# Where partial sums of activations are built, and in which places and order tiles are loaded, in a two-stage f32 matmul kernel

## The reference, cut to what matters

```python
w = weight[adapter_ids]                        # one 2048x2048 matrix for each of the 8 batches
x = x + einsum('bsi,boi->bso', x, w)           # called x1 below
h = einsum('bti,bir->btr', x, lora_A[slot])    # 16 columns
x = x + einsum('bti,oi->bto', x, W) + b + 2 * einsum('btr,bro->bto', h, lora_B[slot])
```

## Time and profile before

| | before |
|---|---|
| median of 3 runs (range) | 2672.59 us (2669.78 to 2679.78) |
| the profiled execution: its time, its span | 2670.25 us, 2668.5 us |
| PE busy | 2573.8 us, 96% of the span |
| DVE, ACT, POOL busy | 1664.3, 876.2, 1247.3 us |
| mean granted clock of PE | 0.988 |
| DMA traffic | 648.03 MB, 243 GB/s in the mean |

### The profile page before, as it was taken

One profiled execution on the slowest core, in us unless ns is written; L12 is line 12 of the kernel. 1 busy time (PEld: TensorE's weight loads), 2 busy tenths in 40 slices (PEclk: granted clock), 3 DMA queues, 4 the chain that ended last, 5 costly groups with the idle time before them and its releaser, 6 DMA issues.

```text
span 2668.5 us, 30970 instructions
## 1 busy us (share of the span) xinstructions
PE 2573.8 (96%) x11232; PEld 2118.8 (79%) x11232; DVE 1664.3 (62%) x1880; ACT 876.2 (33%) x1157; POOL 1247.3 (47%) x1484
## 2 busy tenths in 40 slices
PE   7999999989989999999989989999999999999998
PEld 6887878878878878878878868888888788788776
DVE  5454445444454354453433357899898887999996
ACT  3232232232232242232322324333333333333332
POOL 3333424434434343333322455555666665555665
PEclk9999999999999999999999989999999999999999
DMA  9888888999988878878967894554577955443665
GB/s 336 295 295 269 298 278 262 300 262 290 297 244 308 251 266 321 271 242 264 273 167 194 207 360 148 174 170 163 180 248 262 369 203 172 156 144 131 231 224 192
DMA packets 238155, 648.03 MB, mean 243 GB/s; under 512 B 30132, under 2 KB 46516, under 8 KB 238004
## 3 DMA queue, kind: packets, MB, share of 16 engines
q0 software_dynamic: 124672, 397.48, 46.0%
q1 hardware_dynamic: 113332, 248.57, 28.6%
HBM read 433.07 MB, written 212.86 MB: 242 GB/s over the span
## 4 chain that ended last, share of the span: by engine, by line
PE 86%; DMA 6%; DVE 5%; POOL 1%; issue 1%; ACT 1%; SPq 0%; DVEq 0%; ACTq 0%
PE bank L783 16%; PE bank L785 16%; PE bank L784 16%; PE bank L812 12%; PE bank L814 12%; PE bank L816 12%; DMA x_raw<-xT 3%; DVE x_lo L604 2%; DMA bm<-bs 1%; PE bank L768 1%; PE bank L830 1%; PE bank L769 1%; DVE w_lo L598 1%; DMA wl<-w1s 1%; DVE xc L682 1%
## 5 line engine op out<-in xcount | busy, mean ns | idle before, releaser
L783 PE MATMUL bank<-x_hi,w_hi 128*128 128x512 f32 x2048 | 802.4, 392 | 60.8 <-DVE x_lo L604 60.8
L366 POOL TENSOR_TENSOR wl<-wl 128x512 fp32r<-128x512 f32 x392 | 587.1, 1518 | 459.0 <-ACT wl L532 444.5
L784 PE MATMUL bank<-x_lo,w_hi 128*128 128x512 f32 x2048 | 801.0, 391 | 0.0
L785 PE MATMUL bank<-x_hi,w_lo 128*128 128x512 f32 x2048 | 800.8, 391 | 0.0
L812 PE MATMUL bank<-xc,wl 128*128 128x512 f32 x1568 | 614.9, 392 | 20.4 <-DVE h_mix L617 8.4
L814 PE MATMUL bank<-xc,wl 128*128 128x512 f32 x1568 | 612.2, 390 | 0.0
L816 PE MATMUL bank<-xc,wl 128*128 128x512 f32 x1568 | 611.9, 390 | 0.0
L486 ACT ACTIVATE w_hi<-w_raw 128x1024 fp32r<-128x1024 f32 x256 | 257.5, 1052 | 972.0 <-PE bank L785 961.3
L703 DVE TENSOR_TENSOR x_raw<-bank,x_raw 128x512 f32<-128x512 f32 x128 | 88.5, 691 | 690.3 <-PE bank L785 639.7
L783 PEld LDWEIGHTS bank<-x_hi,w_hi 128*128 128x128 f32 x2048 | 387.0, 189 | 144.0 <-DVE x_lo L604 47.3
L785 PEld LDWEIGHTS bank<-x_hi,w_lo 128*128 128x128 f32 x2048 | 387.0, 189 | 80.9
(11 more groups left out here) (47 smaller groups left out, 1674.4 us busy)
## 6 DMA issues: line engine op xcount, KB each, us to landing
w_raw<-w0T SPq DMA_DIRECT2D x256, 512.0 KB, 7.9
wl<-w1s SPq DMA_DIRECT2D x392, 256.0 KB, 2.7
xss<-x_raw POOLq DMA_DIRECT2D x256, 256.0 KB, 4.2
w1s<-q_raw POOLq DMA_DIRECT2D x196, 256.0 KB, 7.2
q_raw<-w1T POOLq DMA_DIRECT2D x96, 512.0 KB, 9.8
xq<-xss POOLq DMA_DIRECT2D x40, 1024.0 KB, 7.1
x1s<-x_raw POOLq DMA_DIRECT2D x128, 256.0 KB, 2.9
c<-x1s POOLq DMA_DIRECT2D x32, 1024.0 KB, 13.3
```

The costliest lines, as they stand in the source:

```text
L366: pool.tensor_tensor(w[:, 1], w[:, 1].bitcast(F32), w[:, 0].bitcast(F32), ALU.subtract).then_inc(wl_ready, 1)
L783: pe.matmul(sums[s][:], w_hi[s][:, k, :], x_hi[:, k, :], start=(k == 0), stop=False)
L784: pe.matmul(sums[s][:], w_hi[s][:, k, :], x_lo[:, k, :], start=False, stop=False)
L785: mm = pe.matmul(sums[s][:], w_lo[s][:, k, :], x_hi[:, k, :], start=False, stop=(k == KT - 1))
```

## The change

1. **x in nine places.** `x_raw` gets nine chunk places instead of eight (1024 more words per partition, taken from the unused `q_rest`). Chunk 0 of batch 1 is loaded at the start, and every later chunk one place earlier: chunk 7 of the next batch follows tile 13, and after tile 15 comes chunk 0 of the batch after that.
2. **The start.** SP issues all of batch 0's chunks, in turn with the first weights; the second table of slots and the bias follow the weights of tile 1, and POOL's first loads (LoRA A, W) wait for that table and for chunk 6.
3. **The outer sums.** Phase one writes each x1 tile once, and the tiles of the lower half (t >= 8) also negated (`x1n`, 64 stores). `xss` and its 320 writes (160 plain, 160 accumulating) are gone. In phase two each `load_xq` fetches a quadrant of x1, and for five of the seven outer products an accumulating DMA of another 1 MB (`add_xq`) adds the second quadrant, or its negative, into the same SBUF buffer. That makes 40 such loads, four for each of ten outer products; each waits, on POOL, until the plain load has landed, and is issued two pieces after it. Four of them come at the end of phase one.
4. **The border of the phases.** The loads of c0, c1, c2 are spread over pieces 6 to 32 instead of standing in bunches of four at pieces 5, 9 and 13; the last store of h and the waits behind it move from piece 8 to 10 and 17; DVE makes the last low part of h before its first addition into c; PE waits for it at piece m=2 of chunk 1, not at m=0. SP's first `wl` load waits for tile 113's sum as well, since the memory now overlaps `x_raw`.
5. **The end.** The last eight stores (256 KB each) are issued by SP (c0) and ACT (c2) instead of POOL.

The diff, cut:

```diff
-B_SUM = [S6, S7, S1, None, S3, None, S4]
+B_SUM = [(0, 1, False), (2, 3, False), (0, 3, False), (0, None, False), (1, 3, True), (3, None, False), (0, 2, True)]
...
+    XS = XC + 1
...
+    def xq_loads(outer):
+        return sum(1 + (B_SUM[i % OUTER][1] is not None) for i in range(outer + 1))
+
+    def x_rows(b, c):
+        place = (b * XC + c + XC - 1) % XS
+        return slice(place * KX, (place + 1) * KX)
...
+        C_LOADS = {6: (0, 0), 8: (0, 3), 11: (0, 1), 13: (0, 2), 18: (1, 0), 20: (1, 2), 22: (1, 1), 24: (1, 3),
+                   26: (2, 0), 28: (2, 2), 30: (2, 1), 32: (2, 3)}
...
@@ sync
+            b, t = place_of(SEQ // PER_GROUP - 1, 0, INNER_INTO[INNER - 1])
+            for m in range(Q):
+                sp.wait_ge(acc_free, (SEQ - 1) * Q + m + 1)
+                sp.dma_start(yT[b, t + m], c0[:, INNER_INTO[INNER - 1], m]).then_inc(y0_last, 16)
...
@@ gpsimd
+            def add_xq(outer, q):
+                group, o = divmod(outer, OUTER)
+                quad, negative = B_SUM[o][1:]
+                if quad is None:
+                    return
+                pool.wait_ge(xq_loaded[q], (xq_loads(outer) - 1) * 16)
+                b, t = group * 4 + quad % 2 * 2 + q % 2, quad // 2 * HALF + q // 2 * Q
+                source = x1n[b, t - HALF:t - HALF + Q] if negative else x1s[b, t:t + Q]
+                pool.dma_start(xq[q][:], source.rearrange("t p n -> p t n"),
+                               accum_op=ALU.add).then_inc(xq_loaded[q], 16)
...
                     pool.dma_start(x1s[b, t], x1_raw[s][:]).then_inc(x1_stored[s], 16)
-                    for i in BEGINS[quad]:
-                        pool.dma_start(xss[b // 4, i, b % 2, t % HALF], x1_raw[s][:]).then_inc(x1_stored[s], 16)
-                    for i in ADDS[quad]:
-                        pool.dma_start(xss[b // 4, i, b % 2, t % HALF], x1_raw[s][:],
-                                       accum_op=ALU.add).then_inc(x1_stored[s], 16)
-                    for i in SUBTRACTS[quad]:
+                    if t >= HALF:
                         negatives += 1
                         pool.wait_ge(x1_neg_done, negatives)
-                        pool.dma_start(xss[b // 4, i, b % 2, t % HALF], x1_neg[s][:],
-                                       accum_op=ALU.add).then_inc(x1_stored[s], 16)
-                    if b < NB - 1 and t % KX == KX - 1:
-                        load_x(b + 1, t // KX)
+                        pool.dma_start(x1n[b, t - HALF], x1_neg[s][:]).then_inc(x1_stored[s], 16)
+                    if t % KX == KX - 1:
+                        next_b, next_c = divmod(b * XC + t // KX + XS, XC)
+                        if next_b < NB:
+                            load_x(next_b, next_c)
...
                         for q in ((1, 3), (0,), (2,))[j - 3]:
                             load_xq(outer + 1, q)
-                if n == 5:
-                    for i in (0, 3, 1, 2):
-                        load_c(0, 0, i)
-                if n == 8:
-
+                if step == 1 and s >= 0 and outer < SEQ // INNER - 1 and j in (4, 5, 6):
+                    for q in ((1, 3), (0,), (2,))[j - 4]:
+                        add_xq(outer + 1, q)
+                if n == 10:
                     store_h(NB - 1)
+                if n == 17:
+
                     pool.wait_ge(h_stored, NB * 16)
...
@@ scalar
-                    act.wait_ge(xq_loaded[place], (s // INNER + 1) * 16)
+                    act.wait_ge(xq_loaded[place], xq_loads(s // INNER) * 16)
```

More of the change, by code:

```diff
@@ L94, in build @@
     x1s = scratch("x1s", (NB, NT, P, TOK))
-    xss = scratch("xss", (NB // 4, 5, 2, HALF, P, TOK))
+    x1n = scratch("x1n", (NB, HALF, P, TOK))
     w1s = scratch("w1s", (PER_GROUP, Q, P, Q, P))
@@ L98, in build @@
     bs = scratch("bs", (NB, 2, P, HALF * P))
-    def x1_writes(n):
-        quad = n % NT // HALF * 2 + n // NT % 4 // 2
-        return 1 + len(BEGINS[quad] + ADDS[quad] + SUBTRACTS[quad])
     def x1_stores(n):
-        return sum(x1_writes(i) for i in range(n % 2, n + 1, 2))
+        return sum(1 + (i % NT >= HALF) for i in range(n % 2, n + 1, 2))
+    def xq_loads(outer):
[3 more added lines that the diff above has]
+        return slice(place * KX, (place + 1) * KX)
     def xc_sums(until):
@@ L243, in piece, with place_of @@
             return q_raw[u % 3][:, which // 2, which % 2 * Q:(which % 2 + 1) * Q]
+        def place_of(group, quad, i):
+            return group * 4 + quad % 2 * 2 + i % 2, quad // 2 * HALF + i // 2 * Q
+        C_LOADS = {6: (0, 0), 8: (0, 3), 11: (0, 1), 13: (0, 2), 18: (1, 0), 20: (1, 2), 22: (1, 1), 24: (1, 3),
+                   26: (2, 0), 28: (2, 2), 30: (2, 1), 32: (2, 3)}
         q_store = [[(0, 0), (6, 1), (5, 3)], [(1, 3), (4, 2)], [(2, 0)], [(3, 1)]]
@@ L269, in _ @@
                                      .rearrange("a p k o -> (a p) k o")).then_inc(w_loaded[s][part], 16)
+                        if n == 0:
+                            for c in ((2, 3), range(4, XC))[part]:
+                                load_x_first(c)
+                    if n == 1:
+                        sp.dma_start(ids_sb[:, 1, :], ids1).then_inc(ids1_loaded, 16)
+                        sp.dma_start(bias_sb[:], bias).then_inc(bias_loaded, 16)
             def load_bm(i):
@@ L279, in _ @@
             sp.wait_ge(q_stored, UNITS * INNER * 16)
+            sp.wait_ge(x1_sum, TILES - NT + KX)
             for s in range(SEQ):
@@ L367, in wl_lo @@
                                    ).then_inc(wl_ready, 1)
-            for c in range(2, XC):
-                pool.dma_start(x_raw[:, c * KX:(c + 1) * KX], xT[0, c]).then_inc(x_first[c], 16)
-            pool.wait_ge(ids_loaded, 32)
+            pool.wait_ge(ids1_loaded, 16)
+            pool.wait_ge(x_first[XC - 2], 16)
             load_a(0)
             load_q(0)
+            load_x(1, 0)
             negatives = 0
@@ L447, in _ @@
                         pool.wait_ge(x1_stored[i], x1_stores(TILES - 2 + i) * 16)
-                if n in (9, 13):
-                    for i in (0, 2, 1, 3):
-                        load_c(0, (1, 2)[n // 13], i)
+                if n in C_LOADS:
+                    load_c(0, *C_LOADS[n])
                 if step == 1 and s >= 1:
@@ L469, in _ @@
                                                    ).then_inc(y_stored[quad][i], 16)
[L470 to L474, removed]
             for quad in range(4):
@@ L477, in _ @@
                     last = LAST[quad] == OUTER - 1 and INNER_LAST[i] == INNER - 1
-                    pool.wait_ge(y_stored[quad][i], (1 + (Q if last else 1)) * 16)
+                    pool.wait_ge(y_stored[quad][i], (1 if last else 2) * 16)
         @block.scalar
@@ L590, in _ @@
                     h_hi(NB - 1)
+            b, t = place_of(SEQ // PER_GROUP - 1, 2, INNER_INTO[INNER - 1])
+            for m in range(Q):
+                act.wait_ge(acc_free, (SEQ - 1) * Q + m + 1)
+                act.dma_start(yT[b, t + m], c2[:, INNER_INTO[INNER - 1], m]).then_inc(y2_last, 16)
+            act.wait_ge(y2_last, Q * 16)
         @block.vector
@@ L603, in x_lo_part @@
                 dve.wait_ge(x_hi_done, b * XC + c + 1)
-                dve.tensor_tensor(x_lo[:, ks, :], x_raw[:, ks, :], x_hi[:, ks, :].bitcast(F32),
+                dve.tensor_tensor(x_lo[:, ks, :], x_raw[:, x_rows(b, c), :], x_hi[:, ks, :].bitcast(F32),
                                   ALU.subtract).then_inc(x_ready, 1)
@@ L661, in add_terms @@
                     return
-                j, loads = s % INNER, (s // INNER + 1) * 16
+                j, loads = s % INNER, xq_loads(s // INNER) * 16
                 ks = slice(h * (Q // SPLITS), (h + 1) * (Q // SPLITS))
@@ L702, in _ @@
                         dve.wait_ge(x1_stored[s], x1_stores(n - 2) * 16)
-                    dve.tensor_tensor(x1_raw[s][:], sums[s][:], x_raw[:, t, :], ALU.add).then_inc(x1_sum, 1)
+                    row = x_rows(b, t // KX).start + t % KX
+                    dve.tensor_tensor(x1_raw[s][:], sums[s][:], x_raw[:, row, :], ALU.add).then_inc(x1_sum, 1)
                     if n + 2 < TILES:
@@ L726, in _ @@
                 xc_lo(1, h)
+            h_lo(NB - 1)
+            dve.wait_ge(bias_loaded, 16)
             for s in range(SEQ):
@@ L803, in _ @@
                         pe.wait_ge(acc_free, (s - BANK_BEFORE[j]) * Q + m + 1)
-                    if s == 1 and m == 0:
+                    if s == 1 and m == 2:
                         pe.wait_ge(h_ready, NB * (NG // 2))
```

56 lines of the change are left out of this document (26 added, 30 removed).

## The result

The changed kernel takes **2789.7 us** (median of 4 runs, 2786.5 to 2793.2) against 2671.2 before (median of 4 as well): ratio 1.0437, 95% interval 1.0411 to 1.0463. It is 4.4% slower. The forecast was 2738 us, in a range from 2605 to 2800. The profiled execution has a span of 2788.1 us, 119.6 more than before.

A forecast was written before the change was run, and what follows sets the result against it. PE, busy 96% of the span, was taken as the bound, so only its waits could be regained. From 2670.25 us, gains of 55, 5, 5 and 5 (-70) and accumulating-load losses of +138 gave 2738 us, range 2605 to 2800.

The forecast's parts named there:

- Batch borders: Phase one, seven borders where PE waits for x's low part: waits and lower clock vanish, 55 us gained.
- The start: Start of the kernel: first weights land near 8 us instead of 12.8, 5 us gained.
- The border of the phases: Between phases one and two: of 21 us lost, 15 remain or are replaced; 5 gained, ends 0 and 18.
- my 21 us: PE's loss between the phases before the change: waits of 8.4 and 4.7 us, about 8 from the lower clock.
- The end: After DVE's last addition: two queues with one store each save issue time and some landing, 5 us gained.
- The accumulating loads: Nine outer products of phase two: seven lose 14 us each, two at the change of groups 20 each; +138 us.
- time until xq0 is complete: Outer products with accumulating loads: xq0 complete 35.6 us after first issue, needed at 23.9; PE 12 us late.
- the 2 that I gave to the clock: Behind PE's gaps at m=2 and m=3: half clock adds 2 us to 12 us of lateness per outer product.
- The price in engine time: DMA engines in phase two: 1 MB accumulating costs 6.8 us, against 3.1 plain.
- The change of groups: Two outer products where DMA engines are already 0.80 and 0.90 taken: engines are the bound, 20 us lost each.
- stays hidden: Phase two: accumulating loads cost engines what plain ones do, PE does not wait; 2590 to 2625, say 2605 us; chance 0.22.
- lower bound of 22.4 us: Phase two outer products: with accumulating as cheap as plain, xq0 complete at 22.4 us, under the needed 23.9; no loss.

The follow-up runs named there:

- the nine places alone: Kernel before the change, with only the nine chunk places for x and the loads one place earlier: 2613.5 us, ratio 0.979.
- the sums in DRAM: Changed kernel with its third part undone, xss and its 320 stores put back and all other parts kept: 2600.2 us, ratio 0.972.
- without second loads: Changed kernel without the 40 accumulating loads, so five of seven outer products use wrong numbers: 2604.3 us, ratio 0.974.
- with plain ones: Changed kernel with each accumulating load made a plain one of the same bytes, place and waits, overwriting instead of adding: 2691.1 us, ratio 1.006.
- the kernel with q=0 first: Changed kernel with the accumulating loads of q=1 and 3 issued behind that of q=0, in inner chunk 5: 2765.1 us, ratio 1.034.

## Why the prediction was right, and what was mis-sized

**Batch borders**: 55 forecast, 57.5 measured, by the nine places alone. DVE was next, as said: it ended chunk 7's low part at 200.5 in the changed kernel, and PE did not wait:

```profile
199.31 1.22 DVE L640 TENSOR_TENSOR x_lo<-x_raw,x_hi 128x1024 fp32r<-128x1024 f32 x1
```

**The start**: 5 forecast, 4.5 measured. The first weights land at 8.4 us (12.8 before), and LoRA A, landed at 24.4, delays nobody.

```profile
8.40 1.06 ACT L517 ACTIVATE w_hi<-w_raw 128x1024 fp32r<-128x1024 f32 x1 [6.24 <-DMA w_raw<-w0T]
...
24.39 1.34 ACT L530 ACTIVATE a_mix<-a_raw 128x256 fp32r<-128x256 f32 x4 [3.10 <-DMA a_raw<-lora_a]
```

**The border of the phases**: 5 forecast, 3.9 measured, for the reason given. POOL waited 7.0 us for xq2 in front of its accumulating load, c3 came behind it, and DVE stood 15.1 us for c3 (6.3 before):

```profile
1470.76 1.29 POOL L388 DMA_DIRECT2D xq<-x1s  x1 [7.02 <-DMA xq<-x1s]
...
1489.38 2.48 DVE L781 TENSOR_TENSOR c<-bank,c 128x512 f32<-128x512 f32 x4 [15.07 <-DMA c<-x1s]
```

With the sums in DRAM the same stretch is 51.6 us instead of 58.7, and with the nine places alone it is 60.5; so what else the change moves there is worth some 9 where nothing accumulates. One reading in my 21 us was too high: the 8 for the lower clock counts time at that clock in which PE had no matmul (1542 to 1546, at 0.50).

**The end**: 5 forecast, 2.0 measured. The issue of the stores was no longer serial, but the last two still have to land, 6.8 us (SP) and 7.1 (ACT) after their issue in the median.

**The accumulating loads**: this term carried the sign, and it came out right in place and kind: the two gaps at m=2 and m=3, none ahead of outer products 3, 5, 10 and 12, POOL waiting 9.5 to 15.4 us for the plain q=0. It was 138 forecast and 187.5 measured. The **mis-sized term is the time until xq0 is complete**. Step by step, for outer product 1, after the first issue at 1631.2: accumulating q=1 landed at 18.5, accumulating q=3 at 26.0 (the ring free at 21.6 by the forecast), plain q=0 at 29.2 (26), accumulating q=0 at 39.1 (35.6). The last step was priced rightly: 9.5 us from issue to landing here and 9.1 to 9.7 in all nine outer products, where I had 2.3 + 6.8 = 9.1. The 3 us and more come in with the two accumulating loads ahead: q=1 took 12.0 us, and q=3 landed 7.5 after it. In the kernel before, the first matmuls of outer product 1 and of its last piece, m=3 of chunk 6, are 75.3 us apart; here they are 91.6 (m=3 starts at 1674.01, in the row above):

```profile
1623.28 0.39 PE L812 MATMUL bank<-xc,wl 128*128 128x512 f32 x1
...
1698.54 0.39 PE L812 MATMUL bank<-xc,wl 128*128 128x512 f32 x1
```

```profile
1582.42 0.58 PE L849 MATMUL bank<-xc,wl 128*128 128x512 f32 x1
```

So m=3 began 16.3 us late, where I had 12, and the slow matmuls of m=3 cost 2.1 more, as the 2 that I gave to the clock: 18.4 in all, not 14. By this reckoning the slow matmuls of m=2 cost nothing of their own, since m=3 had to wait for xq0 in any case; no run has the waits without the lower clock. Over the seven light outer products the mean is 17.3 and 2.1 (135.8 together, against 98); the 17.3 hold, in some of them, a third gap of 1.9 to 2.7 us ahead of m=2, which I had not seen coming. 5.2 us came in those without such loads.

The price in engine time was not too low but too high. Queue 0 on the page (packets, MB, time as a share of 16 engines' span), of the changed kernel, without second loads, and with plain ones:

```profile
q0 software_dynamic: 113568, 367.06, 40.6%
...
q0 software_dynamic: 92448, 325.11, 34.4%
...
q0 software_dynamic: 103328, 367.06, 37.7%
```

With the spans (2788.1, 2602.7 and 2690.6 us) that is 5.9 us for each of the 40 accumulating loads and 3.0 for a plain one, against 6.8 and 3.1. What I lacked is how much later a load lands when others are under way: why q=1 took 12.0 us and not 9.1 is not shown by any run, beyond that the engines were 94% taken. The DMA share of this outer product is 0.72, where I had said about 0.8.

**The change of groups** (outer products 5 and 6) came out near, 46.3 against 40, but by luck. I had taken the total work of the engines as the bound there, and they are busy 77% and 84% of the time:

```profile
1939.00:2040.20 101.20, 84.45 (x349) 68.18 (x348) 73.81 (x91) 30.71 (x43) 53.16 (x42) 0.92 0.77 237
2040.20:2143.60 103.40, 82.40 (x341) 66.26 (x340) 71.63 (x82) 30.09 (x42) 57.03 (x46) 0.92 0.84 257
```

The gaps stand at m=2 and m=3 as in the light ones, only longer (10.1 and 12.8 us at m=2).

**The rival "stays hidden"** was given 0.22, and that was too much. It rested on a lower bound of 22.4 us that took accumulating q=1 and 3 to be through before the plain q=0 needed the engines. The plain second loads have nearly that bound's price (3.0 us of engine time, 2.6 in the bound), and with them xq0 is complete at 29.2. By the terms of the forecast it would have been 23.0, not 22.4, and so with hardly any room under 23.9. It left out that POOL's wait moves the next issue (13.6 for 12.1), that the plain q=0 lands later with two loads ahead of it (8.8 us, not the 6.6 that it took where none was), and that even 5 us late costs a clock drop.

The rule from the Trainium skill ("DMA: Bandwidth & Descriptors", "Anatomy of one DMA"), about 2.0 us and the bytes at 436 GB/s, puts 1 MB at an estimated 4.4 us. The trace has 5.8 us at least for a plain load and 9.1 at least, 11.5 in the median, for an accumulating one:

```profile
DMA to landing us min/median/max: 9.1/11.5/18.3
```

The measurement decides: for accumulating transfers, here, the rule is too low by a factor of two and more.

What stays open, besides the 12.0 us of q=1: how much of the 46.3 us at the change of groups is owed to the stores and loads of c there; no run here separates them.

## What to carry to other kernels

Price a transfer in DMA-engine time in the stretch where it will run, not by the mean share of its phase: here 39 us at 94% hid in a phase at half load. But engine time alone is not enough: ask when the last transfer of a chain lands. A second transfer that must wait for the first adds its whole latency to the chain and delays what stands behind it in the same ring; moving the waits around changed where PE stands and saved 16 of 185 us. Where a sum can be built as the data is made, with nobody waiting for it, accumulating in DRAM cost nothing that these runs can tell (2600.2 us against 2604.3 without any second term), and the same additions next to their consumer cost 185 us.

## What was not expected of the hardware

An accumulating load of 1 MB into SBUF took 5.9 us of the DMA engines' time, twice the 3.0 of a plain one, and so about what the accumulating stores into DRAM had shown (1.7 us for 256 KB). Three in a row landed at 1657.5, 1663.8 and 1668.9 us in the kernel with q=0 first, 6.3 and 5.1 us apart.

The stretch at the lower clock behind a gap has no fixed length. The gaps of outer product 1, 7.4 and 5.3 us long and 10 us apart, each brought 6.8 us of it. The forecast took 3 to 4 us from the first batch border alone; the third border of the same trace, with a gap of 8.0 us, had already shown more. In these windows around the two the granted clock is 0.86 and 0.79, which makes 3.4 and 6.7 us at half speed (0.14 x 12 and 0.21 x 16, twice):

```profile
208.00:220.00 12.00, 7.22 (x25) 5.44 (x25) 5.67 (x7) 5.29 (x9) 3.20 (x6) 0.86 0.40 158
...
584.00:600.00 16.00, 8.01 (x28) 6.14 (x27) 6.04 (x7) 5.30 (x9) 4.13 (x8) 0.79 0.50 154
```
